# A two-layer attention kernel: another table for the next image's keys and values, and layer 1's first sum split

## What is computed

```python
# layer 0
q, k, v = Wq@xf + bq, Wk@xf + bk, Wv@xf + bv          # 32, 32, 256 rows of n
attn = softmax(q^T k, axis=1)                          # over the rows i of scores[i, j]
x = gamma * (v @ attn) + xf
# layer 1
theta = (theta_w@x + theta_b)^T                        # n x 32
phi, g = maxpool2(phi_w@x + phi_b), maxpool2(g_w@x + g_b)   # 32 x 1024, 128 x 1024
out = (g @ softmax(theta @ phi, axis=-1)^T)            # 128 x n
y = gamma * (out_w@out + out_b) + x
```

## Time and profile before

| | us |
|---|---|
| median of 3 runs | 2818.62 |
| lowest, highest | 2812.73, 2835.16 |
| profiled execution, time | 2825.19 |
| profiled execution, span of its trace | 2823.3 |

### The profile page before, as it was taken

The page is one execution under the profiler, slowest core; times in us unless marked ns, Lnnn a source line. Parts: engine busy times, 40 slices in busy tenths (PEclk is TensorE's granted clock), DMA queues, the critical chain, the costliest instruction groups (busy, mean ns, idle before and its releaser), DMA issues. The chain is left out here.

```text
span 2823.3 us, 38494 instructions
## 1 busy us (share of the span) xinstructions
PE 2650.4 (94%) x11696; PEld 2087.8 (74%) x11696; DVE 2053.1 (73%) x3326; ACT 1744.4 (62%) x3174; POOL 1977.3 (70%) x1551
## 2 busy tenths in 40 slices
PE   6999999989899999988999999998899899999988
PEld 5777777767667777776767777777676677777755
DVE  7677778767767777876776777786687677777665
ACT  5666666555676666665576666665557665666566
POOL 3677776656887777665698777775569777777667
PEclk9999999999999999999999999999999999999988
DMA  2000000110110000011022000001002100000011
GB/s 86 1 16 16 23 23 16 30 38 16 66 63 23 23 23 16 16 38 30 16 70 73 23 16 16 16 23 45 16 8 83 60 16 16 16 16 16 23 38 68
DMA packets 46840, 87.40 MB, mean 31 GB/s; under 512 B 5296, under 2 KB 5424, under 8 KB 46640
## 3 DMA queue, kind: packets, MB, share of 16 engines
q1 hardware_dynamic: 46080, 84.16, 9.2%
q10 hardware_dynamic: 560, 0.79, 0.1%
HBM read 51.12 MB, written 33.55 MB: 30 GB/s over the span
## 5 line engine op out<-in xcount | busy, mean ns | idle before, releaser
L616 POOL TENSOR_TENSOR prob_l<-prob,prob_h 128x512 fp32r<-128x512 f32 x1280 | 1655.4, 1301 | 753.1 <-PE o_ps L1016 670.4
L670 ACT ACTIVATE prob<-s_ps 128x512 f32<-128x512 f32 x1280 | 766.6, 599 | 889.6 <-PE s_ps L989 836.7
L850 DVE TENSOR_REDUCE mx<-aux 128x1 f32<-128x512 f32 x1160 | 793.1, 685 | 346.7 <-PE aux L1049 340.3
L1015 PE MATMUL o_ps<-prob_l,vh 128*128 128x512 f32 x2304 | 912.6, 396 | 10.1 <-POOL prob_l L616 9.4
L1012 PE MATMUL o_ps<-prob_h,vh 128*128 128x512 f32 x2304 | 919.4, 399 | 1.8 <-issue 1.3
L1016 PE MATMUL o_ps<-prob_h,vl 128*128 128x512 f32 x2304 | 905.8, 393 | 0.0
L812 DVE TENSOR_TENSOR acc<-prob,acc 128x512 f32<-128x512 f32 x1152 | 790.1, 686 | 80.8 <-ACT prob L670 64.4
L673 ACT ACTIVATE prob_h<-s_ps 128x512 fp32r<-128x512 f32 x1280 | 764.1, 597 | 0.0
L989 PE MATMUL s_ps<-queries,keys 128*128 128x512 f32 x1280 | 523.1, 409 | 27.4 <-DMA queries<-nm_turned 27.4
L1015 PEld LDWEIGHTS o_ps<-prob_l,vh 128*128 128x128 f32 x2304 | 437.5, 190 | 119.8 <-POOL prob_l L616 31.0
L1012 PEld LDWEIGHTS o_ps<-prob_h,vh 128*128 128x128 f32 x2304 | 438.2, 190 | 102.3 <-ACT osb L684 8.6
(11 more groups left out here) (124 smaller groups left out, 1840.1 us busy)
## 6 DMA issues: line engine op xcount, KB each, us to landing
xa<-x SPq DMA_DIRECT2D x32, 512.0 KB, 3.7
spill<-xa SPq DMA_DIRECT2D x32, 512.0 KB, 2.8
xa<-spill SPq DMA_DIRECT2D x32, 512.0 KB, 3.7
y<-xa SPq DMA_DIRECT2D x32, 512.0 KB, 2.8
xp<-x SPq DMA_DIRECT2D x29, 512.0 KB, 3.7
queries<-nm_turned SPq DMA_DIRECT2D x256, 1.0 KB
xp<-spill SPq DMA_DIRECT2D x3, 512.0 KB, 4.6
prob<-w_in ACTq DMA_DIRECT2D x1, 640.0 KB, 5.7
```

The source lines that it names most:

```text
L616: nc.gpsimd.tensor_tensor(out=prob_l[:, i, :], in0=prob[:, i, :], in1=prob_h[:, h % RING, :].bitcast(f32), op=ALU.subtract).then_inc(pl_re ...
L670: nc.scalar.activation(prob[:, h % PRING, :], s_ps[s][:, :], ACT.Exp).then_inc(p_ready, 1)
L850: ins = nc.vector.tensor_reduce(out=dst, in_=bank[:, :], axis=AX.X, op=ALU.max)
L1015: mm(o_ps[ct][:, :], value(vh, l, t, ct), prob_l[:, low_at, :], start=False, stop=False)
```

## The change

- The tables of (0, b, 7), b < 3, are new. All of chunk 6's values and half of chunk 7's are made there too, so VALUES0_NEXT keeps one of four jobs. Keys and values use both banks, chunk 6 is rounded ahead of chunk 5, the second rounding of chunk 6 moves from (29, 3) to (25, 1) and has x loaded again for it (X_ORDER has an entry more per image), and the slots of x_slot change with it. The chunk's row job M moves from (27, 3) to (28, 1).
- The scores, exponentials and splits of the next image's first chunk begin no earlier than two steps ahead of it (SOFT); for the scores and exponentials it was three.
- In the other chunks of layer 0 the last of the 32 maxima goes from (25, 3) to (25, 1); on X1 the steps 9 and 13 are new and 18 (17) is gone. In (0, b, 0), b > 0, layer 1's maxima start at step 3 instead of 8.
- In layer 1 the first sum is two operations: step 0 copies its probabilities into acc, step 1 adds to it.
- In layer 1 job D2 goes from place 1 to place 3 of step 0.
- On VectorE the adds come behind the step's jobs throughout (0, b, 7), b < 3.

```diff
-AHEAD, SPLIT_AHEAD, SUM_AHEAD = 3, 2, 2
+AHEAD, SPLIT_AHEAD, SUM_AHEAD, SOFT = 3, 2, 2, 2
...
-    X_ORDER += [(0, _b, c) for c in range(NCH)] + [(1, _b, 0)]
+    X_ORDER += [(0, _b, c) for c in (0, 1, 2, 3, 4, 6, 5, 7)] + [(2, _b, 6), (1, _b, 0)]
 X_USE = {use: i for i, use in enumerate(X_ORDER)}
 
 
+def replaced(l, b, n):
+    return l == 0 and n == 0 and b > 0
+
+
 def begin_step(h, ahead):
 
-    return max(h - ahead, GATE if h >= GATE else 0)
+    l, b, n, t = tile_at(h)
+    if h >= GATE:
+        return max(h - ahead, GATE)
+    return max(h - ahead, START[l, b, n] - SOFT if replaced(l, b, n) else 0)
 
 
 def begun_at(g, ahead):
     return [h for h in range(g, min(g + ahead + 1, TILES)) if begin_step(h, ahead) == g]
 
 
-ROUNDS0 = ((2, (10, 1), (10, 3), (11, 1)), (3, (12, 1), (12, 3), (13, 1)), (4, (14, 3), (15, 1), (15, 3)),
-           (5, (18, 1), (18, 3), (19, 1)), (6, (22, 1), (22, 3), (23, 1)), (7, (24, 1), (24, 3), (25, 1)))
-KEYS0 = ((0, (1, 1), X1, (2, 1)), (1, (2, 3), X1, (3, 3)), (2, (11, 3), X1, (12, 3)), (3, (15, 1), X1, (16, 1)),
-         (4, (18, 1), X1, (19, 1)), (5, (19, 3), X1, (20, 3)), (6, (23, 1), X1, (24, 1)), (7, (25, 1), X1, (26, 1)))
-VALUES0 = ((0, 0, (4, 1), X1, (5, 1)), (0, 1, (4, 3), X0, (5, 3)), (1, 0, (8, 1), X0, (9, 1)),
-           (1, 1, (9, 1), X1, (10, 1)), (2, 0, (13, 1), X0, (14, 1)), (2, 1, (13, 3), X1, (14, 3)),
-           (3, 0, (16, 3), X1, (17, 3)), (3, 1, (17, 1), X0, (18, 1)), (4, 0, (20, 1), X0, (21, 1)),
-           (4, 1, (21, 1), X1, (22, 1)), (5, 0, (28, 1), X0, (29, 1)), (5, 1, (28, 3), X1, (29, 3)))
-VALUES0_NEXT = ((6, 0, (1, 1), X1, (2, 1)), (6, 1, (2, 3), X1, (3, 3)), (7, 0, (4, 1), X1, (5, 1)),
-                (7, 1, (5, 3), X1, (6, 3)))
-MAXIMA0 = (((3, 3, X0), (4, 1, X0), (6, 1, X0), (6, 3, X0)), ((7, 1, X0), (7, 3, X0), (10, 1, X0), (10, 3, X0)),
-           ((14, 3, X0), (15, 1, X0), (15, 3, X0), (16, 1, X0)), ((16, 3, X0), (18, 3, X0), (19, 1, X0), (19, 3, X0)),
-           ((21, 3, X0), (22, 1, X0), (22, 3, X0), (23, 1, X0)), ((22, 3, X1), (23, 3, X0), (24, 1, X0), (24, 3, X1)),
-           ((24, 3, X0), (25, 1, X0), (25, 3, X0), (26, 1, X0)), ((26, 3, X1), (26, 3, X0), (27, 1, X1), (27, 1, X0)))
-MAXIMA1 = ((0, 3, X0), (1, 3, X0), (2, 1, X0), (2, 3, X0), (6, 1, X1), (10, 3, X1), (12, 1, X0), (12, 3, X0))
+ROUNDS0 = ((0, 2, (9, 3), (10, 1), (10, 3)), (0, 3, (11, 1), (12, 1), (12, 3)), (0, 4, (14, 1), (15, 1), (15, 3)),
+           (0, 6, (17, 3), (18, 1), (19, 1)), (0, 5, (20, 3), (21, 1), (21, 3)), (0, 7, (21, 3), (22, 3), (23, 3)),
+           (2, 6, (25, 1), (26, 1), (26, 3)))
+KEYS0 = ((0, (1, 1), X1, (2, 1)), (1, (2, 1), X0, (3, 1)), (2, (12, 1), X1, (13, 1)), (3, (14, 1), X0, (15, 1)),
+         (4, (17, 1), X1, (18, 1)), (6, (21, 1), X0, (22, 1)), (5, (22, 3), X1, (23, 3)), (7, (25, 1), X0, (26, 1)))
+VALUES0 = ((0, 0, (3, 1), X1, (4, 1)), (0, 1, (4, 1), X0, (5, 1)), (1, 0, (6, 3), X0, (7, 3)),
+           (1, 1, (8, 3), X0, (9, 3)), (2, 0, (12, 3), X0, (13, 3)), (2, 1, (13, 3), X1, (14, 3)),
+           (3, 0, (15, 1), X1, (16, 1)), (3, 1, (16, 3), X0, (17, 3)), (4, 0, (18, 3), X0, (19, 3)),
+           (4, 1, (20, 1), X1, (21, 1)), (5, 0, (23, 3), X0, (24, 3)), (5, 1, (24, 3), X1, (25, 3)),
+           (6, 0, (28, 1), X1, (29, 1)), (6, 1, (29, 3), X0, (30, 3)), (7, 0, (30, 1), X1, (31, 1)))
+VALUES0_NEXT = ((7, 1, (1, 1), X1, (2, 1)),)
+MAXIMA0 = ((0, ((6, 1, X1), (6, 1, X0), (7, 1, X1), (8, 1, X0))), (1, ((7, 3, X1), (10, 3, X0), (11, 1, X1), (11, 1, X0))),
+           (2, ((15, 3, X0), (16, 1, X0), (16, 3, X1), (18, 1, X0))), (3, ((18, 3, X1), (19, 1, X1), (19, 3, X1), (20, 1, X0))),
+           (4, ((20, 3, X0), (21, 3, X1), (22, 1, X1), (22, 3, X0))), (6, ((23, 1, X0), (24, 1, X1), (24, 3, X0), (25, 3, X1))),
+           (5, ((26, 1, X1), (26, 1, X0), (26, 3, X1), (26, 3, X0))), (7, ((27, 1, X1), (27, 1, X0), (27, 3, X1), (27, 3, X0))))
+MAXIMA1 = ((0, 3, X0), (1, 1, X0), (1, 3, X0), (2, 3, X1), (3, 3, X0), (4, 3, X1), (5, 1, X1), (5, 3, X0))
...
-            place_maxima(g, of(1, b - 1, NCH - 2, 0)[:3] + of(1, b - 1, 0, 1) + of(1, b - 1, 1, 1)
-                         + of(1, b - 1, NCH - 2, 0)[3:] + of(1, b - 1, NCH - 1, 0),
-                         [(t, 1, X1) for t in (8, 9, 13, *range(17, 30))])
+            place_maxima(g, of(1, b - 1, NCH - 2, 0) + of(1, b - 1, NCH - 1, 0)[:1] + of(1, b - 1, 0, 1)
+                         + of(1, b - 1, 1, 1) + of(1, b - 1, NCH - 1, 0)[1:],
+                         [(t, 1, X1) for t in (3, 5, 7, 9, 13, *range(17, 28))])
             put(g + 22, 1, Job("M", 1, b - 1, 0, 0))
             put(g + 26, 1, Job("M", 1, b - 1, 1, 0))
         elif not last_of_image:
-            steps = sorted([(t, 3 if t else 1, X0) for t in range(26) if t not in (3, 6)]
-                           + [(t, 1, X1) for t in (8, 11, 14, 18 if n else 17, 22, 23, 24, 25)], key=lambda e: e[:2])
+            steps = sorted([(t, 3 if t else 1, X0) for t in range(25) if t not in (3, 6)]
+                           + [(t, 1, X1) for t in (8, 9, 11, 13, 14, 22, 23, 24, 25)], key=lambda e: e[:2])
...
-            for c, at, *low_at in ROUNDS0:
-                put(g + at[0], at[1], Job("X", 0, b + 1, c, 0))
+            for r, c, at, *low_at in ROUNDS0:
+                put(g + at[0], at[1], Job("X", r, b + 1, c, 0))
                 for k in range(CT):
-                    put(g + low_at[k][0], low_at[k][1], Job("XL", 0, b + 1, c, k))
-            second_layer(g, *prev[1:], (5, 1), ((5, 3), (6, 3)), (7, 1), (8, 1), (8, 3), (9, 3, X0), (11, 1, X0), (11, 3))
+                    put(g + low_at[k][0], low_at[k][1], Job("XL", r, b + 1, c, k))
+            second_layer(g, *prev[1:], (5, 1), ((6, 1), (6, 3)), (8, 1), (9, 1), (9, 3), (10, 1, X0), (11, 3, X0), (12, 1))
             for c, _, _, low_at in KEYS0:
                 put(g + low_at[0], low_at[1], Job("K0L", 0, b + 1, c, 0))
             values0(g, b + 1, VALUES0)
             for c, at, where, _ in KEYS0:
                 put(g + at[0], at[1], on(Job("K0", 0, b + 1, c, 0), where))
             place_maxima(g, of(1, b, 4, 0) + of(1, b, 5, 0), MAXIMA1)
-            for c in range(KC[0]):
-                place_maxima(g, of(0, b + 1, 0, c), MAXIMA0[c])
-            put(g + 27, 3, Job("M", 0, b + 1, 0, 0))
-            put(g + 29, 3, Job("X", 2, b + 1, NCH - 2, 0))
-            for k in range(CT):
-                put(g + 30, 1 + 2 * k, Job("XL", 2, b + 1, NCH - 2, k))
+            for c, slots in MAXIMA0:
+                place_maxima(g, of(0, b + 1, 0, c), slots)
+            put(g + 28, 1, Job("M", 0, b + 1, 0, 0))
...
-                put(g, 1, on(Job("D2", *prev, 0), X0))
+                put(g, 3, on(Job("D2", *prev, 0), X0))
...
-                put(g, 1, on(Job("D2", *first, 0), X0))
+                put(g, 3, on(Job("D2", *first, 0), X0))
...
     if job.l == 2:
-        return 0
-    if job.l == 1:
-        return 0 if job.c == NCH - 1 and job.b + 1 < B else job.c % 2
-    return (0, 1, 1, 0, 1, 0, 1, 1)[job.c] if job.b else job.c % 2
+        return 1
+    return (0, 1, 1, 0, 1, 1, 0, 0)[job.c] if job.l == 0 and job.b else job.c % 2
...
-                use = (l % 2, b, c)
-                if use in X_USE and not (l == 0 and rounded_late(b, c)):
-                    i = X_USE[use] + PSLOTS
-                    if i < len(X_ORDER) and not X_ORDER[i][0]:
+                if (l, b, c) in X_USE:
+                    i = X_USE[l, b, c] + PSLOTS
+                    if i < len(X_ORDER) and X_ORDER[i][0] != 1:
                         load_x(i)
...
+                    if l:
+                        nc.vector.tensor_copy(acc[:, :], prob[:, i, :]).then_inc(acc_done, 1)
+                elif t == 1 and l == 0:
                     nc.vector.tensor_tensor(out=acc[:, :], in0=prob[:, (h - 1) % PRING, :], in1=prob[:, i, :],
                                             op=ALU.add).then_inc(acc_done, 2)
...
-                fresh = t == KT[l] - SUM_AHEAD
-                if not fresh:
+                entries_first = t == KT[l] - SUM_AHEAD or l == 0 and n == NCH - 1 and b + 1 < B
+                if not entries_first:
                     for h in begun_at(g, SUM_AHEAD):
                         add_prob(h)
                 for e in DURING.get(g, ()):
                     entry(e.job)
-                if fresh:
+                if entries_first:
```

More of the change, by code:

```diff
@@ L523, in load_x @@
                 l, b, c = X_ORDER[i]
-                if l:
+                if l == 1:
                     slot, turn = a_slot(0, b, c)
@@ L527, in load_x @@
                 dst, loaded, _ = x_of(l, b, c)
-                source = spill_v if l else x_v
+                source = spill_v if l == 1 else x_v
                 sp.dma_start(dst[:, :, :], source[:, b * CT:(b + 1) * CT, chunk(c)]).then_inc(loaded, 16)
@@ L622, in entry @@
                     r = ROUND[Job("X", l, b, c, 0)]
-                    src = x_of(l % 2, b, c)[0]
+                    src = x_of(l, b, c)[0]
```

(6 more changed lines are left out.)

## The result

| | before | after |
|---|---|---|
| median, us | 2822.42 | 2740.30 |
| lowest, highest | 2812.73, 2835.16 | 2737.45, 2745.31 |
| ratio, with 95% interval | | 0.9708 (0.9665 to 0.9752) |
| span of the profiled execution | 2823.3 | 2739.0 |

What follows compares the result with a forecast made beforehand. TensorE, busy 94% of the span, was taken as the bound, so time could come only from its idle gaps and slow restarts. 38 + 10 + 9 = 57 us off 2825.2 gave 2768, forecast as 2767, range 2738 to 2798.

Steps and rivals of the forecast that it cites:

- a rival in which (0, b, 7) takes 108 us: New tables also shorten the chunk making the next image's keys and values: 39 us less, 2730 us; chance 0.13.
- Layer 1, 38 us: Splitting layer 1's first sum saves 46 us, less 7.5 for layer 0's sums behind the stretches: net 38, ends 20 and 46.
- The race at layer 0's first sum: Behind each layer 1 stretch, VectorE or GpSimd gets in first; half of three places at 5 us counted, -7.5 us.
- D2 a half-step later: Layer 1's denominator transposes behind three matmuls cover the reciprocal's wait, but GpSimd is the limit: 0, ends -2 and +3.
- Maxima at other steps: Ordinary layer 0 chunks: last maximum 1.36 us earlier removes 19 row waits of 0.5 us at step 28: 10 us, ends 6 and 13.
- the 1.3 us by which an ordinary chunk is busy beyond its count: TensorE busy 62.6 us for 61.3 of counted matmuls in layer 0; subtracted when sizing the stalls of (0,1,7).
- The tables, 9 us: Chunk (0,b,7) 121 us instead of 117.8, (0,b+1,0) 71.5 instead of 77.8: 3 us, three times; ends +45 and -15.
- the tight pairs: In (0,b,7), jobs on one bank with under 0.5 us of matmuls' room: 16 before, 19 in the new table, +2.5 us.
- The start two steps ahead: Next image's scores begin two steps ahead instead of three, hidden if the row is in time: 0; can cost 0.5 to 1.5 each.
- the adds' order: VectorE's adds behind the entries in (0,b,7) come a step later, but ScalarE needs them two steps on: 0.
- the reload: Chunk 6 loaded again, one more 512 KB per image with DMA engines 10% busy: 0.
- the rival that the row comes too late: Next image's row misses step 30 of (0,b,7), some 20 us at each of three places: 2828 us; chance 0.07.

Runs made afterwards that it cites:

- both repairs: The changed kernel with the first sum of (0, b, 1), b > 0, split too and the values' remainder (1, 1) moved to (9, 1): 2714.5 us, ratio 0.9615.
- `max(p, p)`: The changed kernel with the copy in layer 1's first sum written as the maximum of the probability tile with itself: 2771.7 us, ratio 0.9818.

## Why the prediction was right, and where it was off

- **That the number lies in the range is luck.** 57 us were worked out and 82 came. The range reached down to 2738 for a rival in which (0, b, 7) takes 108 us, and that chunk took 123. What brought the time down there was a term of 10 us that came out at 42.
- **Layer 1, 38 us: 35.6,** or 38.3 with D2's matmuls put back on their old side of the cut. Right in mechanism and size. The steady chunk has 12.2 us with GpSimd never idle, where ten times 1.24 was worked out. The race at layer 0's first sum went to GpSimd at all three places, not at half of them, and its price is 19 us for three, where 5 each were counted. A stretch without it is 100.1 us, predicted 100.5.
- **D2 a half-step later, 0: about 9 us** by the medians and 7 by the spans, of which the prediction had 3 x 0.7 in the chunks (0, b, 0). The step that failed is "GpSimd is the limit there, so 0". In the steady chunks it holds (12.4 us with D2 at place 1, 12.1 to 12.5 with it at place 3). At the start of a stretch it doesn't: in the first chunk, of 14.2 us, GpSimd was busy for 12.5, and D2 there stands behind the turning of the maxima of the chunk before ("DVE nm_cols", 1.18 us of wait), not behind the reciprocal alone.
- **Maxima at other steps, 10 us: 42 us, with the chunks behind layer 1.** For the row alone the 10 us were about right: 12. The failed step is that I priced only the maximum that moved at the end. The list loses (18, 1) as well, which had 0.50 and 0.16 us of waits and two restarts on it, 30 us over the run. I took the 1.3 us by which an ordinary chunk is busy beyond its count as a fixed cost of the engine. In the kernel after it is 61.9 for a count of 61.3. Most of it was the slow matmuls after stalls: a stall of 0.5 costs 0.8.
- **The tables, 9 us: 7.5** in the pairs of the two profiles, 0.9988 (0.9963 to 1.0014) by themselves. The 7.5 hold what D2's place brought there, its matmuls included; the tables alone gave 3 us away (591.3 against 588.3), part of it at a lower clock. More work and about the same stalls, as predicted: 121.8 us a chunk at the full clock, 123.3 on average, against 121. The waits for GpSimd went, the tight pairs grew, the 1.63 us at (26, 1) stands where the queue was traced to. The 3.0 us at (10, 1) the sum has no term for: it prices new waits behind a maximum or a key's two remainders, not VectorE standing at a key's remainder until ScalarE, behind a reading of values and two exponentials, has rounded that key. The ends given for this part, +45 and -15, don't follow from 108 and 127 us a chunk, which make +48 and -9; nothing else rests on them.
- **The start two steps ahead, the adds' order, the reload: 0.** No wait for the row at step 30 shows in (0, b, 7), and the rival that the row comes too late didn't occur.
- **Between median and profile.** I took nothing off for the profiled execution's 6.6 us over the median, holding that the spread would shrink with the long sums. It did, from 22 us to 8 in four executions each, and to 2 with both repairs.

## What to carry to other kernels

Where VectorE and GpSimd work side by side, look for VectorE operations with two inputs in SBUF. Their longest time tells more than their mean, and one of them in front of a short operation on which TensorE waits can cost five microseconds; a copy into PSUM and an add from there cost 0.7 us more and were never held here.

When an edit moves entries in a table, price each entry that vanishes from its old place by the waits that stand on it, also the small ones: 0.66 us of waits in a chunk of 63.7, repeated over two dozen chunks, was worth 30 us, more than a rebuilt table. And ask of each wait on a bank which operation frees it and what stands ahead of that one in its engine's queue: the bank's count of matmuls says nothing of it.

## What the hardware showed that I had not expected

- The two-input sum, once missed, was held off for as long as GpSimd had its next operation ready: 4.3 to 5.7 us in eight of 64 before, three to four GpSimd operations of about 1.3 us. Each of the eight ends some 0.56 us behind a GpSimd operation with no other ready behind it. With `max(p, p)`, the same tile twice, it is held just the same (4.97 us). The sums with one input in PSUM ran beside the same GpSimd and never were:

```profile
L812 DVE TENSOR_TENSOR acc<-prob,acc x1152: 635/685/697, 75.5 to 2805.9; 128x512 f32<-128x512 f32 x192
```

- A stall of TensorE costs some 0.27 us beyond the idle gap shown: 0.56 us idle made a pair of matmuls 0.83 us late, 0.16 us made one 0.44 us late. Summing the idle gaps of a stage understates what its stalls cost, by a third for the first and by more than half for the second.
- The same wait can cost more in one place than in another: the 3.0 us at (10, 1) stood in all three chunks, and behind two of them the granted clock was 0.50 for 3.4 and 6.8 us; these chunks took 1.7 and 2.7 us longer than the one where it stayed at 1.00.
